# A graph attention layer and a mixture of experts on one core: the first expert tile prepared inside the routing block

## The reference, cut to what matters

```python
def reference(x, src, dst, ...):
    x = x + gat_two_layers(layernorm(x), edges, ...)       # N = 1250 nodes, D = 768
    xf = layernorm(x)
    gw = gates of the best 2 of 4 groups; ew = gates of the best 4 of 8 experts of each group
    combine = gw[:, :, None] * ew                          # 8 of 32 experts for each node
    for each expert e:
        h = gelu(xf @ W1[e] + b1[e])                       # 768 -> 384
        o = h @ W2[e] + b2[e]                              # 384 -> 768
        y = y + o * combine[:, e]
    return x + y
```

## Time and profile before

| what | us |
| --- | --- |
| median of three runs | 1525.05 |
| lowest and highest of them | 1524.69, 1527.17 |
| the profiled execution, first to last instruction | 1518.7 |
| PE busy in it | 1360.8 (90%) |
| DVE busy | 1160.0 (76%) |
| ACT busy | 737.2 (49%) |
| POOL busy | 505.1 (33%) |

### The profile page before, as it was taken

One profiled execution on the slowest core, in us unless ns is written; L12 is line 12 of the kernel. 1 busy time (PEld: TensorE's weight loads), 2 busy tenths in 40 slices (PEclk: granted clock), 3 DMA queues, 4 the chain that ended last, 5 costly groups with the idle time before them and its releaser, 6 DMA issues. The chain is left out here.

```text
span 1518.7 us, 31335 instructions
## 1 busy us (share of the span) xinstructions
PE 1360.8 (90%) x7728; PEld 1135.4 (75%) x7739; DVE 1160.0 (76%) x1823; ACT 737.2 (49%) x1171; POOL 505.1 (33%) x557
## 2 busy tenths in 40 slices
PE   6888888888778889889977999999999999999995
PEld 4555656733223348889967999999999999999995
DVE  6499999899999988858878477555565655888882
ACT  3556465255555553422224455444454544666662
POOL 1000000003333410032324555555465555555563
PEclk9999999799999999999977999999999999999998
DMA  6300001041222214233566987867778876799963
GB/s 233 138 18 9 18 28 61 18 179 61 73 95 63 78 44 141 63 105 106 127 166 216 269 223 204 186 166 170 171 193 205 203 191 159 210 271 273 254 135 49
DMA packets 102255, 211.68 MB, mean 139 GB/s; under 512 B 19318, under 2 KB 58486, under 8 KB 102082
## 3 DMA queue, kind: packets, MB, share of 16 engines
q1 hardware_dynamic: 79186, 142.06, 28.7%
q0 software_dynamic: 22240, 66.69, 22.0%
q10 hardware_dynamic: 784, 2.36, 0.4%
HBM read 164.14 MB, written 54.93 MB: 144 GB/s over the span
## 5 line engine op out<-in xcount | busy, mean ns | idle before, releaser
L992 PE MATMUL ps_o<-prob,h_head 128*97 128x512 f32 (+1 forms) x480 | 187.7, 528 | 51.5 <-DVE prob L934 51.5
L2070 POOL DMA_INDIRECT out_nodes<-y,to_index x92 | 160.1, 1740 | 133.9 <-issue 73.5
L2387 PE MATMUL ps_h<-e_hi,e_xt_hi 128*128 (+1 forms) x546 | 192.6, 353 | 6.3 <-ACT e_xt_hi L2189 3.6
L992 PEld LDWEIGHTS ps_o<-prob,h_head 128*97 128x97 f32 x480 | 73.2, 164 | 165.4 <-issue 89.7
L2372 PE MATMUL ps_y<-e_hi,e_ht_hi 128*128 (+1 forms) x546 | 191.6, 351 | 3.6 <-DVE e_ht_lo L2305 2.2
L2387 PE MATMUL ps_h<-e_lo,e_xt_hi 128*128 (+1 forms) x546 | 184.7, 338 | 0.0
L2372 PE MATMUL ps_y<-e_hi,e_ht_lo 128*128 (+1 forms) x546 | 183.6, 336 | 0.0
L2372 PE MATMUL ps_y<-e_lo,e_ht_hi 128*128 (+1 forms) x546 | 183.5, 336 | 0.0
L2254 DVE TENSOR_TENSOR e_lo<-raw,e_hi (+1 forms) x189 | 175.6, 950 | 7.3 <-ACT e_hi L2197 6.7
L2207 ACT ACTIVATE y<-ps_y,gate 128x768 f32 (+1 forms) x91 | 82.2, 903 | 192.4 <-PE ps_y L2372 124.2
L826 ACT ACTIVATE score<-score,al_col 128x1250 f32<-128x1250 f32 x80 | 106.0, 1335 | 98.4 <-DVE score L877 98.4
(11 more groups left out here) (357 smaller groups left out, 3053.0 us busy)
## 6 DMA issues: line engine op xcount, KB each, us to landing
raw<-in_ew SPq DMA_DIRECT2D x192, 384.0 KB, 5.7
w_room<-rel_dram SPq DMA_DIRECT2D x14, 640.0 KB, 4.6
b_all<-in_eb SPq DMA_DIRECT2D x32, 192.0 KB
al_src<-al_dram SPq DMA_DIRECT2D x1, 5000.0 KB, 14.6
xs<-in_x SPq DMA_DIRECT2D x5, 768.0 KB, 12.5
x_in_t<-in_x SPq DMA_DIRECT2D x10, 384.0 KB, 3.7
out_nodes<-x SPq DMA_DIRECT2D x10, 384.0 KB, 4.2
table<-xf SPq DMA_DIRECT2D x10, 384.0 KB, 2.7
```

The lines of the kernel that those rows point to most:

```text
L992: turn = nc.tensor.matmul(ps_o[u][0:C1 + 1, c, 0:WID[c]], h_head[:, u, t, :], prob[:, t % 2, 512 * c:512 * c + WID[c]], start=(t == 0), st ...
L2070: nc.gpsimd.indirect_dma_start(out, bass.IndirectOffsetOnAxis(to_index[:, w:w + 1], 0), y[:, w, :], None, bounds_check=NP - 1, oob_is_err= ...
L2387: nc.tensor.matmul(ps_h[:, 0:HID], xt_hi[:, c, :], b[:, bass.ds(e % 2, 1), c * HID:(c + 1) * HID] .rearrange("p o m -> p (o m)"), start=(c ...
```

## The change

It has four parts.

1. Routing block, SP and POOL: the loads of expert 1's weights and of the first bias row move ahead of the last two stores of gates. The two gathers read their column of `list_i` in place; the two copies to `index` go.
2. Routing block, the rest: ACT halves W2 of expert 0 and runs a one-column GELU (`gelu_row`). DVE copies the rows of tile 0 and makes their residues, and copies the rows of tile 1. PE turns the rows of tile 0, computes the first product of tile 0 (`first_product`) and turns the rows of tile 1. The 26 dummy transposes become 3. The list of expert 2 is only matched there.
3. Expert block: tile 0 has left only bias, GELU and transposes. The lists of experts 2 and 3 are written by `keep_early(0)` and `keep_early(1)`; the latter, its product (`list_third`) and the list of expert 4 (`list_fourth`) stand behind the products of tile 1.
4. POOL now waits for `early_kept` 2 ahead of its first index copy in the expert block, and for `early_kept` 4 where it waited for `third_kept` 2.

```diff
...
+        ps_o = [s.ps_first, ctx.enter_context(nc.psum_tensor("ps_mix1", [P, 2, 512], F32))]
         ps_x = ctx.enter_context(nc.psum_tensor("ps_xf", [P, 2, 512], F32))
...
-                store_gates(NT - 2)
-                store_gates(NT - 1)
+                sp.wait_ge(mixed, NT)
+                load_bias(sp, s, b1, 0)
                 for piece in range(3):
                     sp.wait_ge(s.w1_in[piece], 16)
                     load_first(sp, s, w1, 1, piece)
                 for piece in range(3):
                     sp.wait_ge(s.w2_in[piece], 16)
                     load_second(sp, s, w2, 1, piece)
+                store_gates(NT - 2)
+                store_gates(NT - 1)
+                sp.wait_ge(s.b1_in, 16)
+                load_bias(sp, s, b1, 1)
                 for u in range(2):
...
-                pool.wait_ge(list_kept, 1)
-                nc.gpsimd.tensor_copy(s.index[:, :], s.list_i[:, LEAD:LEAD + 1]).then_inc(index_set, 1)
                 for u in range(2):
                     pool.wait_ge(xf_out[u], 16 * (NT // 2))
                 pool.wait_ge(gates_out, 16 * NT)
                 pool.wait_ge(filled, 5)
-                pool.wait_ge(index_set, 1)
+                pool.wait_ge(list_kept, 1)
                 nc.gpsimd.indirect_dma_start(s.landing[:, 0, :], None, s.table.ap(),
-                                             bass.IndirectOffsetOnAxis(s.index[:, 0:1], 0),
+                                             bass.IndirectOffsetOnAxis(s.list_i[:, LEAD:LEAD + 1], 0),
                                              bounds_check=NP - 1, oob_is_err=False).then_inc(s.gathered, 16)
                 pool.wait_ge(list_kept, 2)
-                nc.gpsimd.tensor_copy(s.index_1[:, :], s.list_i[:, LEAD + 1:LEAD + 2]).then_inc(index_set, 1)
-                pool.wait_ge(index_set, 2)
                 nc.gpsimd.indirect_dma_start(s.landing[:, 1, :], None, s.table.ap(),
-                                             bass.IndirectOffsetOnAxis(s.index_1[:, 0:1], 0),
+                                             bass.IndirectOffsetOnAxis(s.list_i[:, LEAD + 1:LEAD + 2], 0),
                                              bounds_check=NP - 1, oob_is_err=False).then_inc(s.gathered_1, 16)
...
-                for t in range(NT - 2, NT):
-                    split_gates(t)
-                    keep_bias(t)
+                for piece in range(3):
+                    act.wait_ge(s.w2_in[piece], 16)
+                    at = piece * PIECE
+                    nc.scalar.activation(s.e2_hi[:, 0, at:at + PIECE], s.raw2[:, 0, at:at + PIECE], ACT.Copy)
+                split_gates(NT - 2)
+                keep_bias(NT - 2)
+                split_gates(NT - 1)
+                nc.scalar.activation(gelu_row[:, :], half_neg[:, :], ACT.Gelu)
+                act.wait_ge(s.x_turned, 1)
+                nc.scalar.activation(s.xt_hi[:, :, :].rearrange("p (b k) n -> p b (k n)", b=2),
+                                     s.ps_first[:, :, 0:HALF], ACT.Copy).then_inc(s.x_hi_made, 1)
+                keep_bias(NT - 1)
...
+                def keep_rows(k, landed):
+                    dve.wait_ge(landed, 16)
+                    nc.vector.tensor_copy(s.in_rows[:, :], s.landing[:, k, 0:D]).then_inc(s.rows_kept, 1)
...
-                rest_of_gates(NT - 2)
-                rest_of_weights(0)
                 start = dve.value_load(s.starts[0:1, 1:2], min_val=LEAD, max_val=LIST - NT)
                 keep(1, start)
+                rest_of_gates(NT - 2)
+                keep_rows(0, s.gathered)
+                rest_of_weights(0)
+                rest_of_weights(1)
+                rest_of_weights(2)
+                dve.wait_ge(s.x_hi_made, 1)
+                nc.vector.tensor_tensor(s.xt_lo[:, :, :].rearrange("p (b k) n -> p b (k n)", b=2),
+                                        s.ps_first[:, :, 0:HALF],
+                                        s.xt_hi[:, :, :].bitcast(F32).rearrange("p (b k) n -> p b (k n)", b=2),
+                                        ALU.subtract).then_inc(s.x_lo_made, 1)
+                rest_of_gates(NT - 1)
+                keep_rows(1, s.gathered_1)
                 match(2)
-                rest_of_gates(NT - 1)
-                rest_of_weights(1)
-                start = dve.value_load(s.starts[0:1, 2:3], min_val=LEAD, max_val=LIST - NT)
-                keep(2, start)
-                rest_of_weights(2)
...
+                def turn_x(k):
+                    pe.wait_ge(s.rows_kept, k + 1)
+                    if k:
+                        pe.wait_ge(s.x_lo_made, k)
+                    for c in range(KD):
+                        last = nc.tensor.transpose(s.ps_first[:, c // 3, (c % 3) * P:(c % 3 + 1) * P],
+                                                   s.in_rows[:, c * P:(c + 1) * P], s.ident[:, :])
+                    last.then_inc(s.x_turned, 1)
+
...
+                def first_product():
+
+                    pe.wait_ge(s.x_hi_made, 1)
+                    for b in (s.e1_hi, s.e1_lo):
+                        for c in range(KD):
+                            if b is s.e1_lo and c % 2 == 0:
+                                pe.wait_ge(w1_lo_ready, c // 2 + 1)
+                            nc.tensor.matmul(s.ps_h[:, 0:HID], s.xt_hi[:, c, :], b[:, 0, c * HID:(c + 1) * HID],
+                                             start=(c == 0 and b is s.e1_hi), stop=False)
+                    pe.wait_ge(s.x_lo_made, 1)
+                    for c in range(KD):
+                        last = nc.tensor.matmul(s.ps_h[:, 0:HID], s.xt_lo[:, c, :],
+                                                s.e1_hi[:, 0, c * HID:(c + 1) * HID],
+                                                start=False, stop=(c == KD - 1))
+                    last.then_inc(s.h_summed, 1)
...
                 turn_gates(NT - 1)
-                turn_nothing(nc, s, ps_l[:, 0:P], 8)
+                turn_x(0)
+                turn_nothing(nc, s, s.ps_h[:, 0:P], 3)
+                first_product()
+                turn_x(1)
                 weigh_bias(NT - 1)
-                list_now(2)
-                turn_nothing(nc, s, ps_l[:, 0:P], 18)
...
+                if start:
+                    with eng.If(tiles > 1):
+                        one(e, 1, early=True)
...
+                pool.wait_ge(early_kept, 2)
                 next_index(LEAD + 2).then_inc(index_set, 1)
...
-                pool.wait_ge(third_kept, 2)
+                pool.wait_ge(early_kept, 4)
...
+                def first_tile():
+
+                    split_x(1)
+                    act.wait_ge(biased, 1)
+                    nc.scalar.activation(h_act[:, :], h_in[:, :], ACT.Gelu).then_inc(gelued, 1)
+                    act.wait_ge(h_turned, 1)
+                    nc.scalar.activation(ht_hi[:, :, :].rearrange("p k n -> p (k n)"), ps_t[:, 0:HID],
+                                         ACT.Copy).then_inc(h_hi_made, 1)
+                    weights(1, 0)
+                    weights(1, 1)
...
-                split_x(0)
-                weights(0, 1)
-                n = over_tiles(act, "act_tiles", tile)
+                act.sem_inc(w2_hi_made, 3)
+                n = over_tiles(act, "act_tiles", tile, first_alone=lambda: None)
...
+                def add_bias(k, e):
+                    dve.wait_ge(h_summed, k + 1)
+                    nc.vector.tensor_tensor(h_in[:, :], ps_h[:, 0:HID],
+                                            b1_all[:, bass.ds(e % BRING, 1), :].rearrange("p o m -> p (o m)"),
+                                            ALU.add).then_inc(biased, 1)
+
...
+                def first_tile():
+
+                    dve.wait_ge(b1_in, 16)
+                    add_bias(0, 0)
+                    keep_early(0)
+                    split_x(1)
+                    rest_of_h(0)
+                    match(AHEAD - 2, 1, early_made)
+                    weights(0, 1, (0,))
+
+                def second_tile(k, e):
+
+                    add_bias(k, e)
+                    keep_early(1)
+                    keep_rows(2)
+                    weights(0, 1, (1, 2))
+                    match(AHEAD - 1, 2, rows_made)
+                    split_x(2)
+                    keep_rows(3)
                     weights(1, 0, range(3))
+                    keep(0)
                     match(AHEAD, 3, rows_made)
-
-                def tile(k, e, which, start, last):
+                    weights(1, 1, (0, 1))
+                    rest_of_h(1)
+                    weights(1, 1, (2,))
+
...
+                def keep_early(n):
+
+                    at = AHEAD - 3 + n
+                    start = dve.value_load(s.starts[0:1, at:at + 1], min_val=LEAD, max_val=LIST - NT)
+                    dve.wait_ge(early_listed, n + 1)
+                    mark_padding(nc, s, ps_l).then_inc(early_kept, 1)
+                    dve.wait_ge(early_kept, 2 * n + 1)
+                    keep_list(nc, s, ps_l, start).then_inc(early_kept, 1)
+                    dve.wait_ge(early_kept, 2 * n + 2)
...
```

(31 more changed lines are left out.)

144 lines of the change are left out of this document (71 added, 73 removed).

## The result

The changed kernel took 1534.84 us (median of 7 runs, 1532.11 to 1538.9), the kernel before 1526.73 us beside it (7 runs, 1521.13 to 1529.0). The ratio is 1.0064, 95% interval 1.0050 to 1.0077: **slower by 0.64%**, 7.6 to 11.8 us. Forecast: 1533.0 us, range 1524 to 1538.

The account below looks back on a forecast made before the run. PE was taken to set the pace in the expert block (busy 120.00 of 120.00 us). Lag 9.6 us at product 3, 1.6 given back, makes +8 on 1518.7; with 6.35 from span to median, 1533 us, range 1524 to 1538.

Parts of the forecast that it names:

- the chain from the list of expert 3 over POOL's queue to the gates of tile 2: Expert block: list written at 823.3, then 3.6 us of POOL queue work and the copy; gates kept at 827.2 us.
- the larger step: Expert block: W1's residues wait behind tile 3's rows and gates, so product 2 starts at 838.4, 7.8 us later.
- This and the earlier weight loads cost nothing on the path: Routing block: first gather without index copy and earlier weight loads are free; bound 0 to 2 us of earlier landing.
- My other branch, POOL's first scatter: Expert block: tile 3's gates also need this scatter, behind the last bias scatter; 834.7 us, same as by gather 3.
- "worse" rival: Expert block: low clock after idle stretches and slow gathers make it worse than forecast, 1537 us; chance 0.11.
- its two conditions: Low clock in every product after an idle stretch (five, 2.2 us each, two on the path); gathers at 8.3 us.
- lies 6.35 us above its span: Whole kernel before: median time exceeds the profiled span of 1518.7 by 6.35 us, added to reach 1533.
- The rule on the table load: Routing block, ACT: skill page's 2.66 us per switch, 1.38 of it drain; block's end 1.1 us later, total 1534.
- The gain stands: Expert block: gates 2 and 3 come in time, only the 4.2 us gain counts, 1521 us; chance 0.12.
- the two cancel: Expert block: W1's residues ready early, lag 2.7 us minus 1.95 given back, 1526 us; chance 0.08.
- It doesn't do what it says: Routing block: late gathers and ACT's last copy move its end to 817, product 1 gains only 2 us, 1535; chance 0.05.

Follow-up runs that it names:

- the later wait: Changed kernel with POOL's wait for `early_kept` 4 moved from ahead of its register loads to the index copy in the loop; ratio to the kernel before 1.0047.

## Why the prediction was right, and where not

The direction, the chain of waits and the time were right; two terms were mis-sized, and the base that the sum was set on was not what I took it for. By its steps, with 2.83 us (794.31 - 791.48) taken off the moments of the changed trace:

| step | forecast | measured |
| --- | --- | --- |
| gather 0 issued | 797.5 | 800.2 |
| rows of tile 0 copied, end | 802.9 | 804.8 |
| product 0 starts | 806.8 | 807.3 |
| expert block starts (DVE) | 814.7 | 814.05 |
| product 1 | 817.6 | 816.3 |
| list of expert 3 written | 823.3 | 822.2 |
| gates of tile 2 kept | 827.2 | 826.4 |
| second product of tile 0 | 829.8 | 829.0 |
| gather 3 issued | 829.0 | 829.1 |
| gates of tile 3 kept | 834.7 | 837.1 |
| product 2 | 838.4, +7.8 | 840.9, +10.3 |
| product 3, lag | +9.6 | +13.0 |
| left of the lag further on | +8 | +11.0 at tile 10 |

**Right:** the chain from the list of expert 3 over POOL's queue to the gates of tile 2. From the writing of the list to the kept gates it took 4.2 us (825.01 to 829.19) where I had 3.6 and a hand-over. Moving the wait showed that it is a real part, worth 2.2 us at tile 10. Also right: that the residues of W1 behind the rows of tile 3 are the larger step; moving them was worth 3.6 us.

**Mis-sized, gather 0.** "This and the earlier weight loads cost nothing on the path": gather 0 was issued 2.7 us late, released by the stores of the gates, which I had not seen as queued behind the loads. I had a bound of 0 to 2 us of *earlier* landing; the row copy was 1.9 us later. The loss was hidden twice. ACT's table load ended before the rows were turned (`e_xt_hi` waited 0.59 us for PE), so it was off the path where I had it on; and product 0 ran partly at the clock of 2.4 GHz (its last 12 products took 2.10 us, 812.13 to 814.23), 4.1 us in all where I took 5.4. That the clock rose there is luck of the execution: in the other versions product 0 took 3.2 to 5.6 us.

**Mis-sized, gather 3.** I took 5.5 us from issue to landing; it was 8.0 (831.91 to 839.91), at the upper end of my bounds. That is all of the difference at product 2 (10.3 against 7.8). My other branch, POOL's first scatter, came out as forecast (POOL was through with it at 834.5, forecast 834.7), and so did not come last. The change didn't slow this gather: in the second profile of the kernel before it took 7.8 us (822.06 to 829.83). With 2.7 of the 5.9 us of product 2 due to the low clock, the forecast's "worse" rival had its two conditions fulfilled, and the trace at tile 10 shows its size, +11.0.

**Missed:** the loop's pace, 1.4 to 2.1 us. And in this profile the last product took 4.6 us instead of 3.1, with its products 0.32 us apart against 0.18, though it stands behind the same wait of 2.17 us in both kernels:

```profile
1518.23 0.44 PE L2464 MATMUL ps_y<-e_hi,e_ht_hi 128*128 128x384 f32 x1 [2.17 <-DVE e_ht_lo L2400]
...
1521.30 0.52 PE L2464 MATMUL ps_y<-e_lo,e_ht_hi 128*128 128x384 f32 x1
1521.62 0.52 PE L2464 MATMUL ps_y<-e_hi,e_ht_lo 128*128 128x384 f32 x1
```

```profile
1501.41 0.44 PE L2372 MATMUL ps_y<-e_hi,e_ht_hi 128*128 128x384 f32 x1 [2.17 <-DVE e_ht_lo L2305]
...
1502.03 0.34 PE L2372 MATMUL ps_y<-e_hi,e_ht_hi 128*128 128x384 f32 x1
1502.21 0.34 PE L2372 MATMUL ps_y<-e_lo,e_ht_hi 128*128 128x384 f32 x1
```

That this belongs to the change is not shown: the wait is 2.17 us in all 14 traces, and the slow last product is in 7 of the 12 with the change.

**Why the time was still right.** The two profiles differ by more than the times: by 11.0 us at tile 10, 11.9 at tile 20, 14.0 at tile 90 and 15.7 from the anchor to the end (11.4 against the second profile), where the ratio makes 9.8 us. The spans of the other executions show why. The profile of the kernel before was one of its quickest (1518.7 us, the median of 65 others 1522.5), and that of the changed kernel was the slowest of 7 (1537.2 us, the others 1530.4 to 1536.3, the median of the 7 1533.1). The medians of the spans differ by 10.6 us. I set the sum against a median that "lies 6.35 us above its span". Of these 6.35 some 4 were the quick execution. The rest is time outside the span, 2.0 to 4.5 us in those 65 executions, median 2.4; in all 7 of the changed kernel it is 1.7. Why it is less there is open. So the delay was about 10 us where I had 8, an underestimate by 2 us and not by the 7.7 that the first two profiles suggest. The range was wide enough for that, and a base taken from medians kept the luck of the first profile out of the sum.

**The rule on the table load.** It took 1.28 us, and the one-column GELU started 1.30 us after it (807.17, 808.47). The Trainium skill, page ScalarE: Activation LUTs, section What ACT_TABLE_LOAD costs, has 1.38 us of drain on top; no row here shows it, and the 1.1 us that I held open for it are not to be found.

**The rivals.** "The gain stands" and "the two cancel" fall with the trace. "It doesn't do what it says" by late gathers: the gather was late, the block's end was not.

## What to carry to other kernels

A wait that moves behind a product takes everything queued behind it along, on its own engine and then on each engine that waits for that one; follow the queue, not the data. When one hold is removed, name the next one before counting the gain: here residues, register work, scatters and loads stood one behind the other, and nearly each edit gave less than it promised. Compare traces from a common instruction ahead of the change, and take a second profile of the kernel before, since one profile may be its luckiest, and one of the changed kernel its unluckiest; the spans of the other runs tell.

## What the runs showed of the hardware that I had not expected

- A gather of 128 rows took 4.0 to 4.7 us from its issue to the copy of its rows with no weights on the way, 7.2 us with six pieces of weights landing beside it, and beside scatters 8.0 in the changed kernel (8.2 in the version with the later wait, 7.8 in the second profile of the kernel before). Whether the stores of gates or the loads went first hardly moved the moment when the rows were copied (13.3 or 12.75 us from the anchor); with the loads behind the gathers it was 10.8.
- The same products ran at 337 to 339 instead of 336 ns (medians of the three kinds) when buffers and blocks of code had moved, in every one of the twelve versions that have the change; 40 tiles took 295.1 to 295.6 us in these, 293.6 and 293.7 in the two profiles without it. The cause is open.
- Behind one and the same wait of 2.17 us the last product of the kernel took 3.1 us in 7 traces and 4.6 in the other 7: the clock that a product meets behind a wait was not the same from one execution to the next.
- 18 dummy products did not carry the clock of 2.4 GHz over a wait of 3.3 us behind them: product 2 again took 5.85 us to the next turning. With 36 products right up to its start it took 3.2 us.
